# State-space stage as one list over batches with split halves and a composed rank product, and three score slots beside four auxiliary banks in the small-head stages

## The reference, cut to what matters

```python
x = hidden_states @ W_in_x.T
z = hidden_states @ W_in_z.T
x_act = silu(causal_conv4(x) + conv_b)          # 512 channels
params = x_act @ W_param.T                       # 128 | 512 | 512
delta = softplus(params[..., :128] @ W_dt.T + b_dt)      # 32 heads
A_bar = exp(delta * A); Bu = delta * B_raw * x_act
h = A_bar * h + Bu                               # scan over tokens
y = (C_raw * h + D * x_act) * silu(z)
return y @ W_out.T
```

## Time and profile before

| What | us |
|---|---|
| median of 3 runs | 4,807.85 (4,805.87 to 4,968.28) |
| profiled execution, its own time | 4,810.19 |
| its span | 4,808.4 |
| TensorE busy | 3,955.8 (82%) |
| VectorE busy | 2,659.3 (55%) |
| ScalarE busy | 1,612.7 (34%) |
| GpSimd busy | 1,238.0 (26%) |

### The profile page before, as it was taken

The page is one execution under the profiler, slowest core; times in us unless marked ns, Lnnn a source line. Parts: engine busy times, 40 slices in busy tenths (PEclk is TensorE's granted clock), DMA queues, the critical chain, the costliest instruction groups (busy, mean ns, idle before and its releaser), DMA issues.

```text
span 4808.4 us, 44217 instructions
## 1 busy us (share of the span) xinstructions
PE 3955.8 (82%) x15840; PEld 2531.9 (53%) x15840; DVE 2659.3 (55%) x4441; ACT 1612.7 (34%) x2226; POOL 1238.0 (26%) x996
## 2 busy tenths in 40 slices
PE   4677958887978883888888868999688788869999
PEld 3455824444754432555565547888433323247887
DVE  4665346664546652768787756333466665545333
ACT  1223235553325550232333223222244343433222
POOL 2004322212421102332323224443111010034442
PEclk8788978898989996899999989999767676679999
DMA  1001000001000001100000010000000000010000
GB/s 53 0 0 40 1 28 1 1 1 36 4 21 1 9 5 76 27 18 25 18 25 18 24 48 24 24 20 1 14 1 1 1 1 1 1 51 20 27 12 18
DMA packets 31948, 83.13 MB, mean 17 GB/s; under 512 B 6400, under 2 KB 7552, under 8 KB 31360
## 3 DMA queue, kind: packets, MB, share of 16 engines
q1 hardware_dynamic: 31744, 80.44, 5.4%
HBM read 59.44 MB, written 4.19 MB: 13 GB/s over the span
## 4 chain that ended last, share of the span: by engine, by line
PE 56%; DVE 21%; ACT 3%; POOL 2%; issue 2%; DMA 1%; SPq 1%; DVEq 0%; POOLq 0%; ACTq 0%
PE ps L226 10%; PE ps L227 10%; PE ps L228 10%; DVE max_cols L1068 6%; PE ps L1022 6%; PE ps L1003 4%; PE ps L1854 3%; PE ps L544 2%; DVE q_lo L2031 2%; PE ps L1016 2%; DVE max_cols L2047 2%; PE ps L998 1%; PE ps L1008 1%; PE ps L735 1%; PE ps L999 1%
## 5 line engine op out<-in xcount | busy, mean ns | idle before, releaser
L1068 DVE TENSOR_REDUCE max_cols<-ps 128x1 fp32r<-128x512 f32 x1024 | 635.9, 682 | 330.9 <-PE ps L1003 190.4
L1047 ACT ACTIVATE probs<-ps 128x1024 f32<-128x1024 f32 x512 | 503.7, 1024 | 353.4 <-PE ps L1016 252.9
L689 POOL TENSOR_TENSOR h_lo<-h,h_hi 128x512 fp32r<-128x512 f32 x304 | 391.9, 1289 | 819.8 <-ACT h_hi L769 819.8
L846 DVE TENSOR_TENSOR gated<-silu,ps 128x512 f32<-128x512 f32 x288 | 198.1, 688 | 693.1 <-PE ps L228 671.0
L1003 PE MATMUL ps<-k_stack,q_stack 64*128 64x512 f32 (+1 forms) x1024 | 405.4, 532 | 159.3 <-DVE max_cols L1068 59.8
L763 ACT ACTIVATE silu<-ps 128x512 f32<-128x512 f32 x304 | 181.8, 598 | 932.7 <-PE ps L228 932.6
L226 PE MATMUL ps<-xn_hi,w_hi 128*128 128x512 f32 x1216 | 481.3, 396 | 0.0
L227 PE MATMUL ps<-xn_lo,w_hi 128*128 128x512 f32 x1216 | 477.3, 392 | 0.0
L228 PE MATMUL ps<-xn_hi,w_lo 128*128 128x512 f32 x1216 | 476.5, 392 | 0.0
L1022 PE MATMUL ps<-probs,v_aug 128*32 128x512 f32 x2048 | 366.7, 796 | 1.9 <-ACT probs L1047 1.9
L1003 PEld LDWEIGHTS ps<-k_stack,q_stack 64*128 64x128 f32 (+1 forms) x1024 | 180.3, 224 | 334.6 <-ACT probs L1047 166.6
(11 more groups left out here) (461 smaller groups left out, 7613.2 us busy)
## 6 DMA issues: line engine op xcount, KB each, us to landing
raw<-in_w_ffn SPq DMA_DIRECT2D x76, 448.0 KB, 3.3
raw<-raw SPq DMA_DIRECT2D x256, 64.0 KB, 2.0
composed_inputs<-in_m_latent SPq DMA_DIRECT2D x1, 5120.0 KB, 15.8
raw<-in_w_mamba SPq DMA_DIRECT2D x8, 448.0 KB, 6.2
raw<-in_w_latent SPq DMA_DIRECT2D x5, 448.0 KB, 17.1
x<-in_x SPq DMA_DIRECT2D x1, 2048.0 KB, 8.5
gated_pattern<-gated SPq DMA_DIRECT2D x4, 512.0 KB, 3.1
raw<-gated_pattern SPq DMA_DIRECT2D x4, 512.0 KB, 4.2
```

Source lines behind the costliest of these rows:

```text
L689: nc.gpsimd.tensor_tensor(HL[:, b % 3, :], hb[:, b % 2, :], HH[:, b % 3, :].bitcast(F32), ALU.subtract).then_inc(G.sem, G.step((s, ev)))
L846: nc.vector.tensor_tensor(ga if routed(i) else hb[:, i % 2, :], sg[:, i % 2, :], bank[2 + i % 2], ALU.mult).then_inc(V.sem, V.step((s, "ga ...
L1047: nc.scalar.activation(self.PB[:, n % 4, :, :], ps[n % 2][:, :, :], ACT.Exp, scale=self.scale).then_inc(A.sem, A.step((s, ("exp", n))))
L1068: nc.vector.tensor_reduce(self.MB[:, self.tile_of(g, h) % 2, q, col:col + 1], self.psum(ev), op=ALU.max, axis=AX.X, negate=True).then_inc( ...
```

## The change

- State-space stage: the loop over batches is written out as one list of events that all engines walk through, with the front of later batches placed among the scans of the present one. All auxiliary products go around banks 0 to 3, B and C around banks 4 to 7. High halves of u and y are made by ScalarE, their low halves and both halves of xn by GpSimd. `u` and `y` have two buffers, z one of its own.
- The rank product is composed: at the start TensorE multiplies the two weights (`wrank`, now among the constants, and `wdt`), and the step sizes of the 32 heads come from u with three products of halves for each tile of it. W_param's other rows are stored as `wb` and `wc`; the packed weights have 8 pieces where they had 9.
- GpSimd cuts only the pieces of wx before the first norm's halves, the others after them, and TensorE waits for pieces one by one.
- max(0, .) of softplus is a Relu on ScalarE. The layer norm is that of the other stages (`front_*`).
- Small-head stages: a score slot is one bank with one head; three slots (banks 0 to 2), four auxiliary banks (3, 4, 5, 7), an exponential for each head.

```diff
+            AUX, PARAM = (0, 1, 2, 3), (4, 5, 6, 7)
+            front = ("mean", "squared", "var", "dev", "xn", "xn cut")
+            events = [(kind, 0) for kind in front] + [("wx", 0, m) for m in every] + [("conv", 0, m) for m in every]
+            events += [(kind, 1) for kind in front[:4]]
+            for b in range(NB):
+                near, far = b + 1 < NB, b + 2 < NB
+                events += [("u", b, m) for m in every] + [("u cut", b, m) for m in every] + [("wz", b, m) for m in every]
+                if near:
+                    events += [("xn", b + 1), ("xn cut", b + 1)]
+                events.append(("steps", b))
+                if b:
+                    events += [("out", b - 1, 0), ("out", b - 1, 1)]
+                events += [("B", b, 0), ("one", b)]
+                events += [("wx", b + 1, 0), ("conv", b + 1, 0)] if near else []
+                events += [("C", b, 0), ("delta", b)]
+                events += [("wx", b + 1, 1)] if near else []
+                events.append(("B", b, 1))
+                events += [("wx", b + 1, 2)] if near else []
+                events.append(("C", b, 1))
+                events += [("wx", b + 1, 3)] if near else []
+                events += [("step", b, 0), ("step", b, 1)]
+                events += [("conv", b + 1, 1)] if near else []
+                events += [("scan", b, 0), ("y cut", b, 0)]
+                events += [("mean", b + 2), ("squared", b + 2)] if far else []
+                events += [("B", b, 2), ("step", b, 2), ("C", b, 2)]
+                events += [("conv", b + 1, 2)] if near else []
+                events += [("scan", b, 1), ("y cut", b, 1)]
+                events += [("var", b + 2)] if far else []
+                events += [("B", b, 3), ("step", b, 3), ("C", b, 3), ("scan", b, 2), ("y cut", b, 2)]
+                events += [("conv", b + 1, 3)] if near else []
+                events += [("scan", b, 3), ("y cut", b, 3)]
+                events += [("dev", b + 2)] if far else []
+            events += [("out", NB - 1, 0), ("out", NB - 1, 1)]
...
+            readers = {"mean": (V, None), "var": (V, None), "wx": (A, None), "wz": (A, None), "steps": (A, None),
+                       "step": (V, "du"), "out": (V, None)}
+            order = [ev for ev in events if ev[0] in readers]
+            aux_no = {ev: n for n, ev in enumerate(order)}
+            def psum(ev):
+                return bank[AUX[aux_no[ev] % len(AUX)]]
+            def param(ev):
+                return bank[PARAM[(ev[2] * 2 + (ev[0] == "C")) % len(PARAM)]]
...
+            def pool(pool, s):
+                stage_start(pool, s)
+                early = (W.whole("wx").stop - 1) // RAWW + 1
+                cut_pieces(pool, dests[:early], first[s])
+                for ev in events:
+                    kind, b = ev[:2]
+                    if kind == "xn cut":
+                        before = [(V, V.at((s, ("xn", b))))]
+                        if b:
+                            before.append((PE, PE.at((s, ("wz", b - 1, MT - 1)))))
+                        cut(pool, s, ev, XH[:, :, :], XL[:, :, :], xc[:, :, :], before)
+                        if b == 0:
+                            cut_pieces(pool, dests[early:], first[s] + early)
+                    elif kind == "u cut":
+                        m = ev[2]
+                        pool.wait_ge(A.sem, A.at((s, "u hi", b, m)))
+                        nc.gpsimd.tensor_tensor(UL[:, m, :], u[:, b % 2, m, :], UH[:, m, :].bitcast(F32),
+                                                ALU.subtract).then_inc(G.sem, G.step((s, ev)))
+                    elif kind == "y cut":
+                        m = ev[2]
+                        pool.wait_ge(A.sem, A.at((s, "y hi", b, m)))
+                        nc.gpsimd.tensor_tensor(YL[:, m, :], y[:, m % 2, :], YH[:, m, :].bitcast(F32),
+                                                ALU.subtract).then_inc(G.sem, G.step((s, ev)))
...
+                        old = order[aux_no[ev] - len(AUX)]
+                        count, mark = readers[old[0]]
+                        count_at = count.at((s, (mark,) + old[1:])) if mark else count.at((s, old))
+                        pe.wait_ge(count.sem, count_at)
...
+                    elif kind == "steps":
+                        if b == 0:
+                            pe.wait_ge(V.sem, V.at((s, "rate lo")))
+                        for k in range(MT):
+                            pe.wait_ge(G.sem, G.at((s, ("u cut", b, k))))
+                            last = mm3(psum(ev)[0:MH, :], WDH[:, k, :], WDL[:, k, :], UH[:, k, :], UL[:, k, :], k == 0, k == MT - 1)
+                        last.then_inc(PE.sem, PE.step((s, ev)))
...
+                    elif kind in ("B", "C"):
+                        m = ev[2]
+                        if b == 0 and m == 0:
+                            pe.wait_ge(G.sem, loaded(s, "w" + kind.lower()))
+                            if kind == "B":
+                                pe.wait_ge(V.sem, V.at((s, "rate lo")))
+                        old = before_of(b, m, 2)
+                        if old:
+                            pe.wait_ge(V.sem, V.at((s, ("bu" if kind == "B" else "y1",) + old)))
+                        for k in range(MT):
+                            wh, wl = w("w" + kind.lower(), k, m)
+                            last = mm3(param(ev), wh, wl, UH[:, k, :], UL[:, k, :], k == 0, k == MT - 1)
+                        last.then_inc(PE.sem, PE.step((s, ev)))
...
+                    elif kind == "u":
+                        m = ev[2]
+                        act.wait_ge(V.sem, V.at((s, ("conv", b, m))))
+                        nc.scalar.activation(u[:, b % 2, m, :], u[:, b % 2, m, :], ACT.Silu).then_inc(A.sem, A.step((s, ev)))
+                    elif kind == "u cut":
+                        m = ev[2]
+                        act.wait_ge(A.sem, A.at((s, ("u", b, m))))
+                        if b and m == 0:
+                            act.wait_ge(PE.sem, PE.at((s, ("C", b - 1, MT - 1))))
+                        nc.scalar.activation(UH[:, m, :], u[:, b % 2, m, :], ACT.Copy).then_inc(A.sem, A.step((s, "u hi", b, m)))
+                    elif kind == "wz":
+                        m = ev[2]
+                        act.wait_ge(PE.sem, PE.at((s, ev)))
+                        if b:
+                            act.wait_ge(V.sem, V.at((s, ("gated", b - 1, m))))
+                        nc.scalar.activation(zs[:, m, :], psum(ev), ACT.Silu).then_inc(A.sem, A.step((s, ev)))
...
+                    elif kind == "y cut":
+                        m = ev[2]
+                        act.wait_ge(V.sem, V.at((s, ("gated", b, m))))
+                        if b and m == 0:
+                            act.wait_ge(PE.sem, PE.at((s, ("out", b - 1, KD - 1))))
+                        nc.scalar.activation(YH[:, m, :], y[:, m % 2, :], ACT.Copy).then_inc(A.sem, A.step((s, "y hi", b, m)))
...
-        AUXB = (4, 5, 7)
+        AUXB = (3, 4, 5, 7)
+        SCORES = (0, 1, 2)
...
-                self.PB = alloc("probs", [P, 4, 2, L])
+                self.PB = alloc("probs", [P, 8, L])
...
-                    for pair in (0, 1):
+                    for h in range(4):
                         if n < len(units):
-                            events.append(("s",) + units[n] + (pair,))
-                        events += at[pair]
+                            events.append(("s",) + units[n] + (h,))
+                        here = at[h // 2]
+                        events += here[len(here) // 2:] if h % 2 else here[:len(here) // 2]
...
-                return bank[AUXB[self.aux_no[ev] % 3]]
-            def step_no(self, g, kt, pair):
-                return (g * QT + kt) * 2 + pair
+                return bank[AUXB[self.aux_no[ev] % len(AUXB)]]
+            def step_no(self, g, kt, h):
+                return (g * QT + kt) * 4 + h
+            def scores(self, n):
+                return bank[SCORES[n % len(SCORES)]]
             def free(self, s, ev, by_act, by_vec):
-                if ev[0] in self.reader and self.aux_no[ev] >= 3:
-                    old = self.order[self.aux_no[ev] - 3]
+                if ev[0] in self.reader and self.aux_no[ev] >= len(AUXB):
+                    old = self.order[self.aux_no[ev] - len(AUXB)]
                     (by_act if self.reader[old[0]] is A else by_vec).append((s, old))
             def pe(self, pe, s, ev, stacked):
...
-                    if n >= 2:
-                        by_act.append((s, ("exp", n - 2)))
+                    if n >= len(SCORES):
+                        by_act.append((s, ("exp", n - len(SCORES))))
...
-                    for i in (0, 1):
-                        h = pair * 2 + i
-                        r = slice((h % self.per) * self.rows, (h % self.per + 1) * self.rows)
-                        last = nc.tensor.matmul(ps[n % 2][:, i, :], self.k_of(g, self.k_tile_no(g, h))[r, kt * P:(kt + 1) * P],
```

(8 more changed lines are left out.)

427 lines of the change are left out of this document (193 added, 234 removed).

## The result

| | before | after |
|---|---|---|
| time, us: median (lowest to highest) | 4,806.9 (4,800.1 to 4,968.3) | 4,663.3 (4,658.5 to 4,669.2) |
| ratio, 95% interval | | 0.9706 [0.9687, 0.9726] |
| profiled execution: span, granted clock | 4,808.4, 0.861 | 4,667.3, 0.871 |

What follows compares the result with a forecast made beforehand. No touched stage fills an engine, so time can only come from waits: 4,810 − 51 (state-space stage) − 58 (small heads) = 4,701, as a median 4,700 us. The forecast's own range was 4,660 to 4,740, the whole range 4,620 to 4,785.

Steps and rivals of the forecast that it cites:

- The cycle: State-space stage: one batch takes 67 us for 81.8, with TensorE idle some 11 us behind ScalarE's SiLUs.
- Contention: State-space stage: GpSimd's weight cuts stretch batch 0's convolutions by 16 us; stage 319, or 303 if only plain two-input operations stretch.
- VectorE gives away the halves: State-space stage: casts and low halves leave VectorE, so some 52 us a batch become 41.
- The bank: Small-head stages: a fourth auxiliary bank shortens the maxima's waits; 60% of 96 us net is taken, −58 us.
- Rotary and pattern: The two small-head stages besides grouped: 1.2 us × 31 groups = 37 us net of the new wait, 60% taken.
- rival A: Small-head stages: head 3's wait eats what the bank frees, bank gives nothing; 4,759 us (4,738 to 4,790), chance 0.19.
- Grouped: Grouped small-head stage: 1.9 us × 31 groups = 59 us net of the new wait, 60% taken.
- The new wait: Small-head stages: each score waits for the exponential of three heads before, up to 0.9 us per unit at low clock.
- rival B: Small-head stages: head 3's wait decides, slower than before; up to +230 us, 4,989 (4,913 at 0.6 us a unit), chance 0.05.
- The third score slot: Small-head stages: cannot pay in itself, since the score product waits only 6.6 us in the grouped stage.
- D: State-space stage: ScalarE's order keeps a batch near 75 us and the bank pays half; 4,761 us, chance 0.06.
- C: Both parts win more: state-space stage 70 us without port contention, small heads 96; 4,644 us, chance 0.2.

Runs made afterwards that it cites:

- x_u_early: Changed kernel with the next batch's root, SiLUs and high halves put on ScalarE ahead of the last scan: 4,653.4 us, state-space stage 297.8.
- x_y_dve: Changed kernel with only the halves of y, not those of u, formed on VectorE: 4,645.9 us, state-space stage 294.4.
- x_late_cuts: Changed kernel with the weight pieces behind the gate's cut after the second batch's input: 4,657.1 us, state-space stage 314.1.
- x_dve_halves: Changed kernel with the high and low halves of both u and y formed on VectorE: 4,652.6 us, state-space stage 303.5.
- x_3aux: Changed kernel with three auxiliary banks instead of four, three score slots and the finer order kept: 4,756.4 us.
- x_4slots: Changed kernel with three auxiliary banks and four single score slots, finer order kept: 4,744.5 us.
- x_2scores: Changed kernel with two single score slots instead of three, four auxiliary banks kept: 4,724.1 us.
- x_pairs: Changed kernel with auxiliary products put between pairs of scores again instead of between single scores: 4,717.5 us.

## Why the prediction was right, and where its steps were off

**State-space stage: −53, forecast −51.** *The cycle* came out as laid out: 66.7 us for 67, a wait of 9.9 us of TensorE for 11, behind the same chain of high half, root, two table loads and SiLUs. x_u_early and x_y_dve show that it is this order that holds the gap open. *Head:* the first projection started at 27.5 for 29. *Contention* was the mis-sized term: I took +16 us for the convolutions of batch 0, they were stretched by 11 (31.1 to 53.5, in x_late_cuts 31.1 to 42.4), since the pieces were cut by 49.4 and the last convolution ran free. `du` of scan 1 started at 99.8 for 107; the last batch took 80 for 78, so that the stage ended 6 us before the 319 of the sum. That the forecast was off by only 2 is in part luck: I had rounded the sum down by 4, with no row behind it. That the convolution steps are held at all, which no row of before showed, is in the rows now, and x_late_cuts takes it away. The Trainium skill's rule ("SBUF — State Buffer", Who interferes with whom) says that two VectorE inputs in SBUF are enough against a GpSimd instruction that reads it, and it holds for the convolution steps here (6.32 us for 2.33). By that rule the sum was 319 and by the narrow reading 303; the trace has 313. The Trainium skill ("ScalarE: Activation LUTs", What ACT_TABLE_LOAD costs) counts a drain with each switch; the measurement differs and decides: the root ends at 121.64, the load stands from 121.66 to 122.94 and the SiLU starts at 122.95, so nothing of it shows.

*VectorE gives away the halves* was the part that I read as a plain gain ("some 52 us a batch become 41"). It is one for u (9.1 us) and a loss for y (18.6). I had priced the order it makes on ScalarE within the cycle, and never asked what the cycle would be without it. What shortened the stage lies between the batches: their first scans are 66.7, 67.4 and 57.9 us apart for 82. That this comes from the one list, which lets batch b+1 run beside batch b, is argued from the trace. x_dve_halves, which keeps the list, the composed rank product, the early start and GpSimd's halves of the input, is at 303.5, 62.5 under the kernel before. Between these four no run tells.

**Small heads: −76, forecast −58.** *The bank* as the part that pays: right, by x_3aux and x_4slots. *Rotary and pattern* together −24 for −22 (60% of 37), in these profiles all of it in rotary. The shown waits don't explain the split: in both stages the new wait ate about what the maxima won (28 us and 23 in rotary, 11 and 16 in pattern), as rival A had it, and rotary is shorter all the same, by 11 us of busy time and 12 of idle time. The pattern stage scatters by 17 us, and its mean of 445 would be a gain of 4. *Grouped* −52 for −35 (60% of 59) is the mis-sized term. I had priced waits alone. Idle time of TensorE fell by 42 us (191 to 149) and its busy time by another 10, at a clock of 0.68 for 0.66, and the 40% that I took off for what VectorE gives back was too much. *The signs* came out: the waits of the maxima are 80.0 us in sum for 159 (forecast some 80), and a unit of the grouped stage is 0.4 us shorter (52 us over 128 units) for 0.5. *The new wait* was 63.9 us in sum over the three stages (scores behind exponentials), under the 100 that would have made the prediction wrong and somewhat over a quarter of rival B's 230. *The third score slot "in itself can't" pay*: right as far as it goes, for x_3aux has three slots without the fourth bank and gains nothing in the grouped and rotary stages. But it left out that the bank needs the slot: x_2scores, with the bank and two slots, loses 61 us of the 90. Nor had I given the finer order a price; x_pairs has it at 54 us.

**Rivals.** A fell with 4,663 (it needed 4,738 or more) and B with the sign; D with a period of 66.7. C (4,644) was nearest in size: 19 us from the measured time, where the forecast's 4,700 is 37 away and its own range of 4,660 to 4,740 holds the result by 3 us. More from the grouped stage was C's half that came, less contention its half that came in part.

**The sum** of the forecast was 4,701 for the profiled 4,669.2, off by 32 us: 2 from the state-space stage, 18 from the heads, 13 from the latent stage, which no edit touches, less 1 from the feed-forward stages.

## What to carry to other kernels

When work is moved to an idle engine, ask first what stands behind it in that engine's order: a copy of 0.6 us that waits for the last scan held up SiLUs that had been ready for 8 us, and TensorE with them. Banks, slots and the order between them are one design: each of the three, undone alone, lost from 54 to 93 us of a gain of 90. And where a stage runs at a clock well below 1, judge an order by busy time as well as by waits: the version with less idle time was the slower one.

## What the runs showed of the hardware

- VectorE's scan with both inputs in SBUF took 1.22 us alone, 1.70 when it began 0.7 us into a low half of 1.3 us on GpSimd (288.66 and 287.98 in the changed kernel) and 2.21 when it began 0.2 us into one (118.69 and 118.53 in x_y_dve). Start and stretch add up to about 1.2 us both times, as if the scan had stood until the low half was nearly done; GpSimd slows down too, four low halves in 6.85 us for 5.03. In x_y_dve a VectorE cast with one input, beside the same low halves, took 1.38 us for 0.43.
- The same 2,552 products of the grouped stage were busy from 619 us (granted clock 0.70) to 707 us (0.63), by the order of the program and from one execution to the next, with 127 to 171 us of idle time in the experiments. The idle time does not tell which is which: x_2scores had the least, and the second longest busy time.
- What decides between those clocks in the grouped stage stays open. The runs change bank counts and order together with the clock, and none holds one while it moves the other.
